# Projection halves issued behind K and Q, context transposes moved to another PSUM bank, and the ScalarE copy of V moved behind a cast

## The chip, the cores and the metric

One core of one Trainium2 chip runs the whole program. The metric is device time in microseconds of that core, as the median of several executions. The engines are TensorE (PE), VectorE (DVE), ScalarE (ACT), GpSimd (POOL), and SyncE (SP), which only issues DMAs here. Each engine works through its own list of instructions strictly in the order in which the program wrote them, and meets the others only at semaphores.

## The reference

The block is a gated cross-attention followed by a gated mixture of experts, over 8 batches of 256 tokens with 128 features. Only the parts that the kernel's order of work depends on are shown.

```
xn = layernorm(layernorm(x))                         # x: (8, 256, 128)
q  = xn @ w_q                                        # 16 heads of 64
k, v = split(ctx_1024 @ w_kv)                        # ctx_1024: (8, 512, 128)
attn = softmax(q * 64**-0.5 @ k.T)                   # per batch and head: 256 x 512
x  = x + tanh(g_xattn) * tanh(gate) * (attn @ v @ w_out + b_out)
t  = layernorm(x)                                    # router, one expert of 8, at most 160 tokens each
x  = x + tanh(g_ffn) * prob * relu(t @ w1[e]) @ w2[e]
```

## The kernel before

Attention runs batch by batch (8), and in a batch pair of heads by pair of heads (8 pairs). One pair is one **slot** of the loop; in the code a slot is `hp`, 0 to 7, and `j` counts slots over all batches. What follows calls them slot 0 to slot 7 of a batch. Each engine has its own function `batch(b)` that writes its instructions for every slot, and those lists are the order of work: nothing is scheduled beyond them.

In slot j, TensorE computes the scores of pair j for two query tiles into two double banks, `psAB` and `psCD` (L1274, or L1267 for the pairs that use a plain fp32 copy: slots 0, 2 and 7). It projects K and Q of pair j+2 into `psEF` (L1193 to L1195), transposes the normalised output of pair j-3 into the end of `psEF` (L1310), projects one eighth of V into `psX` (the same lines), and multiplies values for pair j-2 into `psO` (L1299 to L1301). VectorE takes row maxima (L913, L916), ScalarE the exponentials (L753) and a cast of them to 16 bits (L763), GpSimd the low half of that cast (L654), and SyncE's queue transposes both halves by DMA into `PT` (L477), which the values read two slots later.

Splitting into high and low parts runs through the kernel: ScalarE copies the high part out of PSUM (`kq_hi` L715, `v_hi` L720, `ctxt_hi` L706), and VectorE subtracts it to give the low part (`kq_lo` L900 or L896, `v_lo` L906, `ctxt_lo` L887). `kq_hi` may only start once the transposes L1310 of its slot are done, since they share a bank.

Once per batch there is further work, placed at a fixed slot: the output projection of the batch before in two halves (`project_part` L1353 in slot 1, `project` L1389 in slot 3, both into `psO`, added up on VectorE by `add_part` L957 and `add_attention` L946), the transposes of the next batch's context (`ctx_transposes` L1219, end of slot 2, into `psX`), of the next batch's tokens (slot 4), and the router of the batch before (`tok_transposes` slot 5, `logits` slot 6, `ranks` slot 0 of the batch after, all in `psO`).

`psO` and `psX` each hold one thing at a time. TensorE's `wait_o` and `wait_x` keep for each bank the semaphore that says when its last contents have been read, and make the next writer wait for it: after `project_part` the values wait for `add_part`, after `values` the next writer waits for `normalise_heads` (L924, L930), after a V projection the next waits for `v_lo`. In the program before, VectorE's order in slots 1 and 3 puts `kq_lo` ahead of `add_part` and `add_attention`.

After the last batch's slots comes the rest of the attention and the expert stage, some 50 us.

Of the kernel before, what the change touches and what calls it, by code (L numbers as in the profile page):

```python
# [21 lines left out]
F32 = mybir.dt.float32  # L22
# [11 lines left out]
def gated_block(nc, x, ctx_1024, g_xattn, g_ffn, ln_gamma, ln_beta, w_q, w_kv, w_out, b_out, gate,  # L34
# [34 lines left out]
    with ExitStack() as ctx:  # L69
# [120 lines left out]
        psO = pb("psO", [P, 512])  # L190
        psX = pb("psX", [P, 512])

        def ps_logits(b):
            return (psX if b == B - 1 else psO)[:, 0:QT * E]

        def ps_ranks(b):
            return (psX if b == B - 1 else psO)[:, 0:(QT + 1) * E]

        ps_gw_mid = psO[:, 0:E]

# [114 lines left out]
        def back(b, hp, k):  # L315

            return (b, hp - k) if hp >= k else (b - 1, hp - k + PAIRS)

        def is_last(b):
            return isinstance(b, int) and b == B - 1  # L320
# [65 lines left out]

        def x_bank(b):
            return psO[:, 0:SQ]

        def kq_bank(j):  # L390

# [296 lines left out]
        def _(act):  # L688
# [14 lines left out]

            def ctxt_hi(b):
                act.wait_ge(ctxt_psum, b + 1)
                act.activation(cT_hi[:, b % 2, :], psX[:], ACT.Copy).then_inc(ctxt_hi_done, 1)  # L706

            def kq_hi(b, hp):
                j = b * PAIRS + hp
# [72 lines left out]

            def batch(b):
                for j, hp in slots(b):
                    if hp == CTX_STEP + 1 and not is_last(b):
                        ctxt_hi(b + 1)
                    exps(b, hp, 0)
                    if not (is_last(b) and hp + AHEAD >= PAIRS):
                        kq_hi(*next_pair(b, hp, AHEAD))
                    if hp == CTX_STEP:  # L790
                        v_hi(*v_group(b, hp))
                    if j < LAST:
                        phi(b, hp, 0)
                    exps(b, hp, 1)
                    if ot_pair(j) >= 0:
                        ot_copy(ot_pair(j))
                    if hp != CTX_STEP and v_group(b, hp):
                        v_hi(*v_group(b, hp))
                    if j < LAST:
                        phi(b, hp, 1)  # L800
                    if hp == X_STEP and not is_last(b):
                        xt_hi(b + 1)
                    if hp == LOGITS_STEP and not is_first(b):
                        router_exp(b - 1)
# [32 lines left out]
        def _(dve):  # L837
# [46 lines left out]

            def ctxt_lo(b):
                dve.wait_ge(ctxt_hi_done, b + 1)
                dve.tensor_tensor(cT_lo[:, b % 2, :], psX[:], cT_hi[:, b % 2, :].bitcast(F32), ALU.subtract).then_inc(ctxt_lo_done, 1)  # L887

            def kq_lo(b, hp):
                j = b * PAIRS + hp  # L890
# [176 lines left out]
            def batch(b):  # L1067
                for j, hp in slots(b):
                    row_max(b, hp, 0)
                    if hp == CTX_STEP + 1:  # L1070
                        if not is_last(b):
                            ctxt_lo(b + 1)
                    elif j and v_group(*back(b, hp, 1)):
                        v_lo(*v_group(*back(b, hp, 1)))
                    if hp == RANKS_STEP and b > 1:
                        take_ranks(b - 2)
                    if hp == X_STEP and not is_last(b):
# [15 lines left out]
                    if j == LAST:  # L1093
                        low_parts()
                        place(B - 2)
                    if not (is_last(b) and hp + AHEAD >= PAIRS):
                        kq_lo(*next_pair(b, hp, AHEAD))
                    if hp == CTX_STEP:
                        v_lo(*v_group(b, hp))
                    if hp == PART_STEP and not is_first(b):  # L1100
                        add_part(b - 1, b - 1)
                    if hp == PROJECT_STEP and not is_first(b):
                        add_attention(b - 1)
                    if VALUES_BEHIND <= j < LAST:
                        normalise_heads(*back(b, hp, VALUES_BEHIND))
                    if hp == PROJECT_STEP and not is_first(b):
# [84 lines left out]
        def _(pe):  # L1191
# [22 lines left out]

            def ctx_transposes(b):
                pe.wait_ge(ctx_in, 16 * b + 16)
                wait_x((ctxt_lo_done, b + 1))
                for kt in range(KT):
                    last = pe.transpose(psX[:, P * kt:P * kt + P], ctx_raw[:, kt, :], ident[:])  # L1219
                last.then_inc(ctxt_psum, 1)  # L1220

            def k_project(b, hp):
# [96 lines left out]
                last.then_inc(tokt_psum, 1)  # L1319

            def logits(b):
                (wait_x if b == B - 1 else wait_o)((route, b * ROUTE + 4))
                pe.wait_ge(tokt_done, b + 1)
                pe.wait_ge(gw_mid_done, 1)
                for q in range(QT):
                    last = pe.matmul(ps_logits(b)[:, E * q:E * q + E], tT[:, P * q:P * q + P], gw_mid[:], start=True, stop=True)
                last.then_inc(logit_psum, 1)
# [29 lines left out]
            def ranks(b):  # L1357


                (wait_x if b == B - 1 else wait_o)((route, b * ROUTE + 7))  # L1360
                pe.wait_ge(hot_done, QT * (b + 1))
                if b:
                    pe.wait_ge(route, (b - 1) * ROUTE + 7)
                else:
                    pe.wait_ge(pool_consts, 5)
                carried = taken[:].unsqueeze(1).to_broadcast([P, QT + 1, E])
                pe.matmul(ps_ranks(b).rearrange("p (t e) -> p t e", e=E), ident[:], carried, start=True, stop=False)
                for i, (counts, c) in enumerate(((tri, 2), (ones_bf, 1), (ones_bf, 0))):
                    last = pe.matmul(ps_ranks(b), counts[:], hot_padded[:, c:c + QT + 1, :].rearrange("p t e -> p (t e)"),
                                     start=False, stop=(i == 2))  # L1370
                last.then_inc(pos_psum, 1)
# [51 lines left out]
            def batch(b):  # L1423
                for j, hp in slots(b):
# [6 lines left out]
                        ranks(b - 2)  # L1431
                    if j == LAST:
                        ranks(b - 1)
                    if hp == PART_STEP and not is_first(b):
                        project_part(b - 1, range(PAIRS // 2))
                    if hp == PROJECT_STEP and not is_first(b):
                        project(b - 1)
                    if hp == X_STEP and not is_last(b):
                        x_transposes(b + 1)
                    if hp == TOKT_STEP and not is_first(b):  # L1440
# [5 lines left out]
                    if ahead:  # L1446
                        if is_first(b) and hp == 2:
                            pe.wait_ge(w_lo_rest_done, 3)
                        k_project(*next_pair(b, hp, AHEAD))
                        q_project(*next_pair(b, hp, AHEAD))  # L1450
                    if ot_pair(j) >= 0:
                        if not ahead:
                            pe.wait_ge(kq_done, LAST + 1)
                            pe.wait_ge(ot_done, ot_pair(j))
                        o_transposes(ot_pair(j))
                    if v_group(b, hp):
                        v_project(*v_group(b, hp))
                    if VALUES_BEHIND <= j < LAST:
                        values(*back(b, hp, VALUES_BEHIND))
                    if hp == CTX_STEP and not is_last(b):  # L1460
                        ctx_transposes(b + 1)
                    if j == 0:
                        pe.wait_ge(v_lo_done, 2)
                        keep_busy(6, psO[:, 0:P])
                if is_last(b):
# [5 lines left out]
                    pe.wait_ge(ot_done, LAST - 2)  # L1471
                    o_transposes(LAST - 2)
                    values(b, PAIRS - 2)
                    project_part(b, range(PAIRS // 2, PAIRS - 2), psEF)
                    pe.wait_ge(ot_done, LAST - 1)
                    o_transposes(LAST - 1, psEF[:, 512:1024], 2)
# [112 lines left out]
```

## Time and profile before

| what | value |
|---|---|
| device time, median of 3 (lowest to highest) | 491.48 us (490.69 to 491.77) |
| the profiled execution | 489.88 us, of which its span is 487.9 us |
| TensorE matmul busy | 433.6 us, 89% |
| VectorE, ScalarE, GpSimd busy | 75%, 78%, 73% |
| DMA queue 1, all hardware DMAs | 281600 packets, 77.96 MB, 89.7% of 16 engines |
| granted TensorE clock, mean of the span | 0.994 |

The profile is one execution, so its own time is 1.6 us below the median. A busy share says how full an engine is over the whole span, not whether the end waits for it; where an engine sat idle, the profile names what ended the idle time. In a timeline row the first number is the start in us from the start of the span, the second the time it took, and a bracket gives the idle time just before it and what ended it.

### The profile page before, as it was taken

To read this page: it belongs to the slowest core of one execution; us is meant where nothing else is said; L and a number is where in the kernel's file an instruction comes from. 1 tells how busy PE (TensorE), PEld (TensorE's weight loads), DVE (VectorE), ACT (ScalarE), POOL (GpSimd) and SP (SyncE) were. 2 spreads that over 40 slices of the span, in tenths; PEclk is the share of its full clock that TensorE was granted. 3 is DMA by queue.
4 is the path that set the end of the run, shared out by engine and by line. 5 is a ranking of instruction groups with operands and counts; after the bars stand their busy time and mean duration, and the time that the engine had idled before them with its cause. 6 is when DMAs were issued, how large, how long until landed. Compare 5 with 4: busy or idle time off the path is not lost.

```text
span 487.9 us, 13156 instructions
## 1 busy us (share of the span) xinstructions
PE 433.6 (89%) x5096; PEld 334.3 (69%) x5096; DVE 367.0 (75%) x803; ACT 382.9 (78%) x616; POOL 355.7 (73%) x270
## 2 busy tenths in 40 slices
PE   8869998899889998899889989899889989888893
PEld 7647775676667776676667767677667666657893
DVE  4788886699678886789669887689669867785622
ACT  5879997699778988699788987799779986893330
POOL 3785894788867987798867987788778876681325
PEclk9998999999999999999999999999999999999999
DMA  6399999899998999999989999999989997797021
GB/s 181 128 206 174 184 205 156 162 199 196 194 184 179 193 192 170 187 186 202 190 180 176 179 186 184 195 188 196 190 129 177 192 179 138 124 165 163 14 65 44
DMA packets 283037, 82.10 MB, mean 168 GB/s; under 512 B 264387, under 2 KB 280435, under 8 KB 282976
## 3 DMA queue, kind: packets, MB, share of 16 engines
q1 hardware_dynamic: 281600, 77.96, 89.7%
q0 software_dynamic: 1376, 3.30, 2.1%
q8 instruction: 41, 0.67, 0.6%
q14 instruction: 20, 0.16, 0.1%
HBM read 10.83 MB, written 5.14 MB: 33 GB/s over the span
## 4 chain that ended last, share of the span: by engine, by line
PE 53%; DVE 18%; ACT 12%; DMA 7%; issue 6%; POOL 3%; POOLq 0%; SPq 0%; ACTq 0%; DVEq 0%
DVE MXL L913 7%; DMA PT<-PARTS 6%; PE psO L1299 5%; ACT P L753 4%; PE psAB L1267 4%; PE psO L1301 4%; ACT HL L715 4%; PE psO L1300 4%; PE psAB L1274 4%; PE psCD L1274 3%; DVE HL L900 3%; PE psEF L1193 3%; PE psO L1389 3%; PE psO L1353 3%; PE psEF L1195 2%
## 5 line engine op out<-in xcount | busy, mean ns | idle before, releaser
L654 POOL TENSOR_TENSOR PARTS<-P,PARTS 128x1024 f16<-128x1024 f32 x125 | 267.2, 2140 | 78.3 <-ACT PARTS L763 77.6
L763 ACT ACTIVATE PARTS<-P 128x1024 f16<-128x1024 f32 x126 | 135.3, 1074 | 0.8
L1299 PE MATMUL psO<-VH,PT 128*128 128x65 f16 x1008 | 99.6, 195 | 26.6 <-DVE row L946 11.5
L1299 PEld LDWEIGHTS psO<-VH,PT 128*128 128x128 f16 x1008 | 90.9, 98 | 46.6 <-DVE row L946 14.6
L753 ACT ACTIVATE P<-psAB,NB 128x512 f32<-128x512 f32 x128 | 81.5, 694 | 42.4 <-DVE NB L916 41.1
L1300 PE MATMUL psO<-VL,PT 128*128 128x64 f16 x1008 | 99.0, 193 | 0.0
L1301 PE MATMUL psO<-VH,PT 128*128 128x65 f16 x1008 | 98.8, 194 | 0.0
L913 DVE TENSOR_REDUCE MXL<-psAB 128x2 f32<-128x1024 f32 x64 | 78.3, 1223 | 19.5 <-PE psAB L1274 12.3
L1301 PEld LDWEIGHTS psO<-VH,PT 128*128 128x128 f16 x1008 | 92.0, 97 | 0.0
L1300 PEld LDWEIGHTS psO<-VL,PT 128*128 128x128 f16 x1008 | 91.9, 99 | 0.0
L753 ACT ACTIVATE P<-psCD,NB 128x512 f32<-128x512 f32 x128 | 81.0, 692 | 1.5 <-DVE NB L916 0.7
L913 DVE TENSOR_REDUCE MXL<-psCD 128x2 f32<-128x1024 f32 x64 | 77.6, 1213 | 0.2 <-PE psCD L1274 0.2
L900 DVE TENSOR_TENSOR HL<-psEF,HL 128x768 fp32r<-128x768 f32 x41 | 39.2, 955 | 26.5 <-ACT HL L715 24.7
L715 ACT ACTIVATE HL<-psEF 128x768 fp32r<-128x768 f32 x41 | 33.4, 814 | 19.0 <-PE psEF L1310 18.6
L906 DVE TENSOR_TENSOR VL<-psX,VH 128x512 f16<-128x512 f32 x63 | 42.8, 680 | 1.5 <-ACT VH L720 1.5
L1274 PE MATMUL psAB<-HL 64*128 64x512 f32 x252 | 41.2, 432 | 0.8 <-ACT P L753 0.8
L1274 PE MATMUL psCD<-HL 64*128 64x512 f32 x252 | 37.5, 402 | 4.2 <-ACT P L753 4.2
L720 ACT ACTIVATE VH<-psX 128x512 f16<-128x512 f32 x63 | 38.8, 616 | 0.0
L924 DVE RECIPROCAL rden<-psO 128x4 f32<-128x4 f32 x64 | 11.4, 179 | 35.2 <-PE psO L1301 34.6
L1193 PE MATMUL psX<-w_hi,cT_hi 128*128 128x512 f32 x63 | 30.2, 479 | 5.0 <-DVE VL L906 2.6
L742 ACT ACTIVATE OT<-psEF 128x256 f32<-128x256 f32 (+1 forms) x63 | 25.1, 399 | 9.1 <-PE psEF L1310 7.2
L1274 PEld LDWEIGHTS psCD<-HL 64*128 64x128 f32 x252 | 22.5, 186 | 14.3 <-ACT P L753 10.2
(228 smaller groups left out, 876.5 us busy)
## 6 DMA issues: line engine op xcount, KB each, us to landing
ctx_raw<-in_ctx_dram SPq DMA_DIRECT2D x8, 256.0 KB, 3.6
w1s<-in_L_ffn_w_dram SPq DMA_DIRECT2D x8, 256.0 KB, 3.4
w2s<-in_L_ffn_w_dram SPq DMA_DIRECT2D x8, 256.0 KB, 4.4
PT<-PARTS SPq DMA_TRANSPOSE x126, 4.8
experts_table<-zeros POOLq DMA_DIRECT2D x2, 645.0 KB, 4.1
X<-in_x_dram SPq DMA_DIRECT2D x8, 128.0 KB, 4.0
wraw<-in_L_xattn_w_kv_dram SPq DMA_DIRECT2D x4, 256.0 KB, 5.1
out_dram<-row SPq DMA_DIRECT2D x8, 128.0 KB, 2.8
```

The lines of the kernel that those rows point to most:

```text
L654: pool.tensor_tensor(PARTS[:, par, qt, 1], P32[:, par, qt], PARTS[:, par, qt, 0], ALU.subtract).then_inc(plo_done, 1)
L715: act.activation(HL[:, hp % 2, H_KHI:H_KHI + KQ], kq_bank(j)[:, 0:KQ], ACT.Copy).then_inc(kq_hi_done, 1)
L753: last = act.activation(P32[:, par, qt, SK * h:SK * h + SK], score_bank(qt)[:, SK * h:SK * h + SK], ACT.Exp, bias=NB[:, par, qt, h:h + 1])
L763: act.activation(PARTS[:, hp % 2, qt, 0], P32[:, hp % 2, qt], ACT.Copy).then_inc(phi_done[qt], 1)
L900: dve.tensor_tensor(hl[:, H_KLO:H_KLO + KQ], kq_bank(j)[:, 0:KQ], hl[:, H_KHI:H_KHI + KQ].bitcast(F32), ALU.subtract).then_inc(kq_done, 1)
L906: dve.tensor_tensor(VL[:, kt, 8 * half:8 * half + 8, :], bank[:].rearrange("p (h d) -> p h d", d=DH), VH[:, kt, 8 * half:8 * half + 8, 0:D ...
L913: dve.tensor_reduce(MXL[:, par, qt, :, 0], score_bank(qt)[:].rearrange("p (h n) -> p h n", h=2), AX.X, ALU.max, negate=True).then_inc(max_ ...
L1193: pe.matmul(dst, hi_l, hi_r, start=True, stop=False)
L1274: last = pe.matmul(score_bank(qt)[:, SK * h:SK * h + SK], hl[rows, q + P * qt:q + P * qt + P], hl[rows, k:k + SK], start=(q == H_QHI and k ...
L1299: pe.matmul(psO[:, g:g + DH + 1], phi, VH[:, kt, head, 0:DH + 1], start=first_, stop=False)
L1300: pe.matmul(psO[:, g:g + DH], phi, VL[:, kt, head, :], start=False, stop=False)
L1301: last = pe.matmul(psO[:, g:g + DH + 1], plo, VH[:, kt, head, 0:DH + 1], start=False, stop=last_)
```

## The change

TensorE issues the two projection halves (slots 1 and 3) behind the K and Q projections of the slot rather than ahead of them, and VectorE adds each half ahead of `kq_lo` rather than behind it. The context transposes move from the end of slot 2 to just behind the scores of that slot, and for every batch but the first they go to `psO` rather than `psX`; ScalarE's and VectorE's split of them moves from slot 3 to slot 2. ScalarE's `v_hi` moves behind the cast L763 of the second query tile in every slot, also in slot 2, where it stood between `kq_hi` and the first cast; VectorE's `v_lo` for slot 2 moves to slot 3 as in the other slots. The logits and ranks of the last batch but one go to `psEF`.

```diff
+        def route_bank(b):
+            return {B - 1: psX, B - 2: psEF}.get(b, psO)
...
+        def ctx_bank(b):
+            return psO if b else psX
...
@@ ScalarE, batch(b) @@
-                    if hp == CTX_STEP + 1 and not is_last(b):
+                    if hp == CTX_STEP and not is_last(b):
                         ctxt_hi(b + 1)
                     exps(b, hp, 0)
...
-                    if hp == CTX_STEP:
-                        v_hi(*v_group(b, hp))
...
-                    if hp != CTX_STEP and v_group(b, hp):
-                        v_hi(*v_group(b, hp))
                     if j < LAST:
                         phi(b, hp, 1)
+                    if v_group(b, hp):
+                        v_hi(*v_group(b, hp))
...
@@ VectorE, batch(b) @@
                     row_max(b, hp, 0)
-                    if hp == CTX_STEP + 1:
-                        if not is_last(b):
-                            ctxt_lo(b + 1)
-                    elif j and v_group(*back(b, hp, 1)):
+                    if j and v_group(*back(b, hp, 1)):
                         v_lo(*v_group(*back(b, hp, 1)))
+                    if hp == CTX_STEP and not is_last(b):
+                        ctxt_lo(b + 1)
...
-                    if not (is_last(b) and hp + AHEAD >= PAIRS):
-                        kq_lo(*next_pair(b, hp, AHEAD))
-                    if hp == CTX_STEP:
-                        v_lo(*v_group(b, hp))
                     if hp == PART_STEP and not is_first(b):
                         add_part(b - 1, b - 1)
                     if hp == PROJECT_STEP and not is_first(b):
                         add_attention(b - 1)
+                    if not (is_last(b) and hp + AHEAD >= PAIRS):
+                        kq_lo(*next_pair(b, hp, AHEAD))
...
@@ TensorE @@
-                wait_x((ctxt_lo_done, b + 1))
+                (wait_o if b else wait_x)((ctxt_lo_done, b + 1))
...
-                (wait_x if b == B - 1 else wait_o)((route, b * ROUTE + 4))
+                if b == B - 2:
+                    pe.wait_ge(kq_done, LAST + 1)
+                else:
+                    (wait_x if b == B - 1 else wait_o)((route, b * ROUTE + 4))
...
-                    if hp == PART_STEP and not is_first(b):
-                        project_part(b - 1, range(PAIRS // 2))
-                    if hp == PROJECT_STEP and not is_first(b):
-                        project(b - 1)
+                    if hp == CTX_STEP and not is_last(b):
+                        ctx_transposes(b + 1)
...
                         q_project(*next_pair(b, hp, AHEAD))
+                    if hp == PART_STEP and not is_first(b):
+                        project_part(b - 1, range(PAIRS // 2))
+                    if hp == PROJECT_STEP and not is_first(b):
+                        project(b - 1)
...
-                    if hp == CTX_STEP and not is_last(b):
-                        ctx_transposes(b + 1)
...
+                    pe.wait_ge(route, (B - 2) * ROUTE + 7)
                     project_part(b, range(PAIRS // 2, PAIRS - 2), psEF)
```

## Rows read from the trace of the kernel before

**Rows 1.** Busy time by stretch: slot 1, slot 3, and one whole batch.

```profile
core 0: us, PE busy (x) PEld busy (x) DVE busy (x) ACT busy (x) POOL busy (x), PEclk, DMA share, GB/s
...
177.20:186.00 8.80, 7.15 (x90) 5.96 (x87) 5.59 (x10) 7.08 (x13) 7.42 (x5) 1.00 1.05 181
...
192.90:201.70 8.80, 7.15 (x90) 5.96 (x89) 4.62 (x7) 7.07 (x13) 7.04 (x5) 1.00 1.15 172
...
sum 54.20, PE 49.43 PEld 37.27 DVE 43.14 ACT 45.93 POOL 43.48; mean PE 6.18 PEld 4.66 DVE 5.39 ACT 5.74 POOL 5.43
```

**Rows 2.** Who waited for whom: total us, times, longest.

```profile
PE psO L1299 <- DVE row L946: 11.5, 7, 1.7
PE psO L1299 <- DVE X L957: 11.5, 7, 1.7
...
PE psX L1219 <- DVE VL L906: 3.9, 6, 0.7
...
PE psO L1299 <- DMA PT<-PARTS: 1.7, 4, 0.7
...
PEld psO L1299 <- DVE winners L994: 1.4, 1, 1.4
```

**Rows 3.** Timeline of TensorE, slot 1 of batch 3.

```profile
177.20 0.97 PE L1274 MATMUL psAB<-HL 64*128 64x512 f32 x6
...
178.01 0.86 PE L1274 MATMUL psCD<-HL 64*128 64x512 f32 x6
...
178.80 2.05 PE L1353 MATMUL psO<-wo,OT 128*128 128x128 f32 x16
...
180.60 0.47 PE L1193 MATMUL psEF<-cT_hi,w_hi 128*128 128x512 f32 x1
...
181.88 0.47 PE L1193 MATMUL psX<-w_hi,cT_hi 128*128 128x512 f32 x1
...
184.47 0.20 PE L1299 MATMUL psO<-VH,PT 128*128 128x65 f16 x1 [1.65 <-DVE X L957]
```

**Rows 4.** Timeline of VectorE, the same slot 1.

```profile
183.06 0.96 DVE L900 TENSOR_TENSOR HL<-psEF,HL 128x768 fp32r<-128x768 f32 x1 [1.51 <-ACT HL L715]
183.93 0.47 DVE L957 SCALAR_TENSOR_TENSOR X<-psO,gscale,X 128x256 f32<-128x256 f32 x1
```

**Rows 5.** Timeline of ScalarE, slot 1 and the first exponential of slot 2.

```profile
182.22 0.81 ACT L715 ACTIVATE HL<-psEF 128x768 fp32r<-128x768 f32 x1 [1.29 <-PE psEF L1310]
...
183.87 1.26 ACT L753 ACTIVATE P<-psCD,NB 128x512 f32<-128x512 f32 x2
...
188.63 1.26 ACT L753 ACTIVATE P<-psAB,NB 128x512 f32<-128x512 f32 x2 [1.80 <-DVE NB L916]
```

**Rows 6.** Timeline of TensorE and ScalarE, the context's transposes and copy.

```profile
192.33 0.63 PE L1219 MATMUL psX<-ident,ctx_raw 128*128 128x128 f32 x4 [0.65 <-DVE VL L906]
...
194.25 0.64 ACT L706 ACTIVATE cT_hi<-psX 128x512 fp32r<-128x512 f32 x1
```

**Rows 7.** Timeline of ScalarE, VectorE and TensorE in slot 5: one group of V.

```profile
208.90 0.63 ACT L720 ACTIVATE VH<-psX 128x512 f16<-128x512 f32 x1
...
210.02 0.68 DVE L906 TENSOR_TENSOR VL<-psX,VH 128x512 f16<-128x512 f32 x1
...
211.19 0.47 PE L1193 MATMUL psX<-w_hi,cT_hi 128*128 128x512 f32 x1
```

**Rows 8.** Timeline of SyncE's DMA queue, batches 3 and 4, merged.

```profile
191.59 1.19 SPq L452 DMA_DIRECT2D X<-in_x_dram  x1
...
199.43 0.94 SPq L484 DMA_DIRECT2D ctx_raw<-in_ctx_dram  x1
...
206.11 2.48 SPq L457 DMA_DIRECT2D w1s<-in_L_ffn_w_dram  x2
...
216.03 0.58 SPq L448 DMA_DIRECT2D out_dram<-row  x1
216.71 10.97 SPq L477 DMA_TRANSPOSE PT<-PARTS  x4
...
228.41 16.96 SPq L477 DMA_TRANSPOSE PT<-PARTS  x6
```

More of the change, by code:

```diff
@@ L191, in gated_block @@
         psX = pb("psX", [P, 512])
+        def route_bank(b):
+            return {B - 1: psX, B - 2: psEF}.get(b, psO)
         def ps_logits(b):
-            return (psX if b == B - 1 else psO)[:, 0:QT * E]
+            return route_bank(b)[:, 0:QT * E]
         def ps_ranks(b):
-            return (psX if b == B - 1 else psO)[:, 0:(QT + 1) * E]
+            return route_bank(b)[:, 0:(QT + 1) * E]
         ps_gw_mid = psO[:, 0:E]
@@ L705, in ctxt_hi @@
                 act.wait_ge(ctxt_psum, b + 1)
-                act.activation(cT_hi[:, b % 2, :], psX[:], ACT.Copy).then_inc(ctxt_hi_done, 1)
+                act.activation(cT_hi[:, b % 2, :], ctx_bank(b)[:], ACT.Copy).then_inc(ctxt_hi_done, 1)
             def kq_hi(b, hp):
@@ L886, in ctxt_lo @@
                 dve.wait_ge(ctxt_hi_done, b + 1)
-                dve.tensor_tensor(cT_lo[:, b % 2, :], psX[:], cT_hi[:, b % 2, :].bitcast(F32), ALU.subtract).then_inc(ctxt_lo_done, 1)
+                dve.tensor_tensor(cT_lo[:, b % 2, :], ctx_bank(b)[:], cT_hi[:, b % 2, :].bitcast(F32), ALU.subtract).then_inc(ctxt_lo_done, 1)
             def kq_lo(b, hp):
@@ L1216, in ctx_transposes @@
                 pe.wait_ge(ctx_in, 16 * b + 16)
-                wait_x((ctxt_lo_done, b + 1))
+                (wait_o if b else wait_x)((ctxt_lo_done, b + 1))
                 for kt in range(KT):
-                    last = pe.transpose(psX[:, P * kt:P * kt + P], ctx_raw[:, kt, :], ident[:])
+                    last = pe.transpose(ctx_bank(b)[:, P * kt:P * kt + P], ctx_raw[:, kt, :], ident[:])
                 last.then_inc(ctxt_psum, 1)
@@ L1357, in ranks @@
             def ranks(b):
-                (wait_x if b == B - 1 else wait_o)((route, b * ROUTE + 7))
+                if b == B - 2:
+                    pe.wait_ge(route, b * ROUTE + 4)
+                else:
+                    (wait_x if b == B - 1 else wait_o)((route, b * ROUTE + 7))
                 pe.wait_ge(hot_done, QT * (b + 1))
```

## The prediction, made blind

> **What bounds the kernel now.** I read the busy time by stretch first, then the waits, then the timelines of single slots. A batch takes 54.20 us and TensorE's matmuls fill 49.43 of it at full clock [rows 1], so 4.8 us per batch is all that a better order alone can win. Most of the gap sits in two slots: slots 1 and 3 last 8.80 us each with 7.15 us of matmul, the slots that hold a projection half [rows 1]. The waits name the cause: in seven batches the values wait 1.65 us for `add_part` and as long for `add_attention`, 23.0 us together, and six times the context's transposes wait for `v_lo`, 3.9 us [rows 2].
>
> The timeline of slot 1 shows how that wait comes about. TensorE issues scores, the half, K and Q, the output transposes, V, and then stands until 184.47 [rows 3]. The half was done at 180.85, but VectorE had `kq_lo` first in its list, and that stood 1.51 us for ScalarE's `kq_hi` [rows 4], which stood 1.29 us for the output transposes [rows 5]. So `add_part` started 3.1 us after its operand was there, and held `psO` until 184.40. Slot 3 is built alike.
>
> **The change part by part.** I walk the new order through batch 3, keeping each stretch from start to start as the rows have it.
>
> *Halves behind K and Q, sums ahead of `kq_lo`.* From the first score to the next matmul is 1.60 us, the half takes 1.80 to the next start, K to V 1.28 [rows 3], of which the output transposes, which lie just ahead of V, are 0.14 by the order of the list. So K starts at 178.80, the half at 179.94, the output transposes at 181.74 as before, V at 181.88. The half ends at 181.99; VectorE is idle then (from 183.06 less 1.51, 181.55), so `add_part` runs to about 182.55 and costs nothing ahead of a `kq_lo` that still waits for ScalarE until 183.06 [rows 4]. V needs 0.8 us before the values, so they start at 182.67 and not at 184.47: **1.80 us** won in slot 1. The exponential of the second tile keeps its place, 183.87 to 185.13 [rows 5], and the second scores of slot 2, now due at 185.3, just clear it. Nothing is left over there: ScalarE is next in line.
>
> *Context transposes in slot 2, in `psO`.* The wait of 0.65 us goes with the bank [rows 6], because `psO` was emptied by the normalisation after the values end at 184.3, well ahead of the transposes at 186.1. They last 0.63 us. The new place adds two waits. ScalarE's `ctxt_hi` now stands first in slot 2, and behind it stand all its exponentials, `kq_hi` and casts; it starts when the transposes are done (186.8), which is when ScalarE comes free of slot 1, so I cost the wait at nothing and the copy at 0.64 us [rows 6]. The first exponentials of slot 2 then start near 187.4, still 1.2 us earlier than the 188.63 of before [rows 5]. VectorE's `ctxt_lo` (a 128x512 subtraction like the 0.68 us of `v_lo` [rows 7]) stands ahead of the second row maximum; it ends at 188.2, and the values of slot 2, which need the bank, are due at 188.75: covered, with half a microsecond to spare. Bounds: the transposes' wait of 0.65 gained in full, and on the other side the 0.64 us of the copy and 0.68 us of the subtraction paid in full. I take the gain less what ScalarE costs in the next step, since both waits lie under work.
>
> *Slot 3.* Scores start at 190.3 (before: 192.9). Here ScalarE is late: `kq_hi`, the first cast and the second exponentials of slot 2 end at 191.5, so the second scores stand about 0.4 us. The projection half then repeats slot 1: values at 196.2, slot 4 at 197.75 against 201.7 before. The walk wins **3.95 us** by slot 4.
>
> *`v_hi` behind the second cast.* The sum of ScalarE's work before the next exponentials is the same. The cast, and with it GpSimd's subtraction and the DMA transposes, come 0.5 us sooner; `v_lo` comes later. Slot 5 is the tightest: `v_hi` ran 208.90 to 209.53, `v_lo` from 210.02 to 210.70, V from 211.19 [rows 7]. Put behind a cast of about 1.1 us, `v_hi` ends near 210.5, `v_lo` near 211.25, and V waits some 0.15 us. In slot 2 `v_lo` now comes a slot later, and V of slot 3, behind the half, has room. Bounds per slot: nothing (the other slots) to 1.0 us (the whole move). I take 0.25 us per batch, near the slot-5 row. The walk stands at **3.7 us**.
>
> *Last batch but one's logits in `psEF`.* This removes the one wait of 1.4 us for the routing [rows 2]. But the scores of the last slot then wait for the exponentials before them, which hang on VectorE's maxima, so I count nothing (bounds 0 to 1.4). The added waits are old by the time TensorE gets there.
>
> *What is late next: the DMA queue.* SyncE's queue is not touched in its order, but it is asked to do the same in less time. From 216.71 to 245.37 it issued ten transposes with one load between and no gap worth the name: 28.66 / 10 = 2.87 us each [rows 8]. Sixteen of them are 45.9 us, and the other loads of a batch 1.19 + 0.94 + 2.48 + 0.58 = 5.2 us [rows 8]: **51.1 us** of queue in a batch that now takes 54.20. The walk would need 50.5. So the queue gives out first, at 3.1 us; I take **3.0** and leave the last tenth for transposes that land late.
>
> A transpose moves 128 x 2048 two-byte elements, 524 KB, so 2.87 us is 183 GB/s. The Trainium skill, "DMA: Bandwidth & Descriptors", section "Latency and other measured facts", gives an effective 261 GB/s for such transposes. By that, an estimate, one would take 2.0 us, the queue would need 37 us, and the time would be that of the walk alone. This trace does not agree where the queue is full.
>
> *Sum.* Batches 1 to 7 hold the halves: 7 x 3.0 = 21.0 us. In batch 0 the context's split moves too, but V in slot 3 then waits for `v_lo` where it waited for `ctxt_lo`: nothing. The profiled execution is 489.88 us (span 487.9), which gives 468.9; on the median, 491.48 - 21.0 = **470.5 us**.
>
> **The rivals.** *The queue has room after all.* A transpose that is handed over sooner also drains sooner; the waits for transposed data are only 1.7 us in the whole run [rows 2], which speaks for slack. Then the walk holds, 7 x 3.7 to 7 x 3.95: 464 to 465.6 us. The skill's figure above points this way.
>
> *The queue has less room.* In a batch of 54.20 us the queue stands idle only between some loads and the next transpose, as from 192.78 and from 200.37; if only half the 3.1 us can be used before transposes land behind the values, 7 x 1.55 = 11 us: about 480.5, between 476 and 485.
>
> *ScalarE's chain is the bound.* `kq_hi` still waits for the output transposes (1.29 us [rows 5]), now behind the half as before. If only the 1.25 us by which the first exponentials of slot 2 come earlier survive, 7 x 1.25 = 8.8 us: 482.7.
>
> *Slower: V waits in every full slot.* `v_hi` behind the cast moves `v_lo`, which frees `psX` for the next V. Where TensorE has no gap (slots 0 and 4 to 7, 35 of them), a wait of the whole 1.0 us costs 35 us against 21 won: about 505.5. It decides from 0.6 us per slot. Against it: `v_lo` is held by VectorE's row maximum anyway, and slot 5 shows a shift of about half a microsecond with half of slack.
>
> **How the numbers follow.** Forecast (466 to 476) 0.55; queue with room 0.10; queue with less 0.16; ScalarE's chain 0.08; no effect 0.04; slower 0.07. Faster by over 0.2% (1 us, about what a measurement here can tell from no change) is the first four, 0.89; within 0.2%, 0.04; slower, 0.07. The range 463.5 to 484 takes in both ends of the queue and most of ScalarE's case.
>
> **What would show it.** After: no wait of L1299 on L957 or L946, none of L1219; slots 1 and 3 near 7.0 and 7.5 us; a batch near 51 us; the wait of L1299 on `PT` grown from 1.7 us to several, and the queue's transposes back to back over whole batches. If batches stand at 50.5 with no such wait, the queue had room. If `psCD` scores wait for exponentials over 1 us in slots 2 and 3, ScalarE took the gain. If V waits for `v_lo` by over 0.3 us in slots 4 to 7, the moved copy costs what I held small.

## The result, and the profile after

| what | before | after |
|---|---|---|
| device time, median (lowest to highest) | 491.41 us (490.69 to 491.77) | 469.76 us (468.03 to 470.58) |
| ratio, 95% interval | | 0.9557 (0.9527 to 0.9586) |
| the profiled execution, of which its span | 489.88 us, 487.9 us | 469.92 us, 468.1 us |
| TensorE matmul busy | 433.6 us, 89% | 435.2 us, 93% |
| DMA queue 1, share of 16 engines | 89.7% | 95.7% |

The change made the kernel faster by 4.4%; the forecast of 470.5 us missed the median by 0.7 us. The median of before stands on four executions here; the forecast had three of them. TensorE does the same work in less idle time. The waits of TensorE after (total us, times, longest) answer to [rows 2]:

```profile
PE psO L1300 <- DMA PT<-PARTS: 7.5, 11, 1.9
PE psCD L1275 <- ACT P L759: 5.1, 16, 1.4
PE psX L1194 <- DVE VL L910: 2.7, 2, 2.5
```

The two waits for `add_part` and `add_attention`, 23.0 us, and the 3.9 us of the context's transposes are gone. In their place the values wait for transposed data 7.5 us where they waited 1.7. TensorE's timeline of slot 1 of batch 3 after, against [rows 3]:

```profile
170.64 0.96 PE L1275 MATMUL psAB<-HL 64*128 64x512 f32 x6
...
172.23 0.50 PE L1194 MATMUL psEF<-cT_hi,w_hi 128*128 128x512 f32 x1
...
173.38 1.95 PE L1357 MATMUL psO<-wo,OT 128*128 128x128 f32 x16
175.16 0.38 PE L1311 MATMUL psEF<-ident,O 128*128 128x128 f32 x2
175.30 0.48 PE L1194 MATMUL psX<-w_hi,cT_hi 128*128 128x512 f32 x1
...
176.09 0.20 PE L1300 MATMUL psO<-VH,PT 128*128 128x65 f16 x1
```

No row has a bracket: TensorE does not stand once. Counted from the slot's start, half, V and values begin at 2.74, 4.66 and 5.45 us. VectorE in the same slot, against [rows 4]:

```profile
175.36 0.48 DVE L961 SCALAR_TENSOR_TENSOR X<-psO,gscale,X 128x256 f32<-128x256 f32 x1 [0.22 <-PE psO L1357]
176.49 0.96 DVE L904 TENSOR_TENSOR HL<-psEF,HL 128x768 fp32r<-128x768 f32 x1 [0.64 <-ACT HL L721]
```

The sum starts 0.22 us after VectorE came free, as the half ends, and `kq_lo` behind it still waits 0.64 us for ScalarE: the sum costs nothing there. The busy time by stretch, with the columns of [rows 1], for slots 1, 2 and 3 of batch 3 and then for whole batches 2, 4, 5 and 6:

```profile
170.64:177.60 6.96, 6.96 (x90) 5.94 (x87) 5.78 (x10) 5.22 (x9) 5.08 (x5) 1.00 1.13 186
177.60:183.70 6.10, 6.10 (x76) 4.13 (x73) 5.36 (x9) 6.00 (x11) 5.15 (x3) 1.00 1.06 215
183.70:191.25 7.55, 7.26 (x90) 5.87 (x87) 5.51 (x10) 6.05 (x11) 5.99 (x5) 1.00 1.20 183
...
114.40:164.50 50.10, 49.36 (x609) 37.23 (x607) 43.49 (x94) 45.60 (x74) 43.15 (x32) 1.00 1.16 201
215.20:267.70 52.50, 49.51 (x610) 37.27 (x607) 43.48 (x94) 45.46 (x74) 43.06 (x32) 1.00 1.05 190
267.70:320.30 52.60, 49.78 (x608) 37.28 (x607) 43.56 (x94) 45.91 (x74) 43.26 (x32) 1.00 1.10 194
320.30:370.20 49.90, 49.29 (x606) 36.99 (x605) 43.60 (x94) 45.74 (x74) 43.31 (x31) 1.00 1.09 184
```

The slots are as walked. The batches are not alike: two stand near 50 us, which is TensorE full to 99%, and two stand some 2.5 us longer with the same TensorE work. From the first score of a batch to the next batch's, in us (worked out from the timelines):

| batch | 0 | 1 | 2 | 3 | 4 | 5 | 6 | 7 (seven slots) | its slot 7 to the end |
|---|---|---|---|---|---|---|---|---|---|
| before | 51.8 | 53.5 | 53.8 | 54.2 | 53.9 | 54.0 | 53.7 | 47.8 | 53.2 |
| after | 52.4 | 49.9 | 50.1 | 50.7 | 52.5 | 52.6 | 50.0 | 42.8 | 55.1 |
| gain | -0.6 | 3.6 | 3.7 | 3.4 | 1.4 | 1.4 | 3.8 | 5.1 | -1.9 |

### The profile page after: what moved, and what is told of

The parts are those of the page before. It is cut to its first block, busy times and chain, and to the rows that moved or that the text cites. A ratio compares the mean times of both kernels' runs of the same rounds, so it can differ in the third digit from the quotient of the medians.

```text
span 468.1 us, 13156 instructions
## 1 busy us (share of the span) xinstructions
PE 435.2 (93%) x5096; PEld 333.4 (71%) x5096; DVE 370.1 (79%) x803; ACT 382.5 (82%) x616; POOL 355.7 (76%) x270
## 3 DMA queue, kind: packets, MB, share of 16 engines
q1 hardware_dynamic: 281600, 77.96, 95.7%
## 4 chain that ended last, share of the span: by engine, by line
PE 43%; DVE 14%; DMA 12%; ACT 12%; POOL 11%; issue 6%; POOLq 0%; SPq 0%; ACTq 0%; DVEq 0%
DMA PT<-PARTS 11%; POOL PARTS L660 8%; DVE MXL L917 5%; ACT P L759 5%; DVE HL L904 3%; PE psO L1300 3%; PE psAB L1268 3%; PE psCD L1275 3%; PE psO L1302 3%; PE psO L1301 3%; PE psEF L1194 3%; ACT PARTS L769 3%; PE psO L1396 3%; PE psCD L1268 3%; ACT HL L721 2%
## 5 line engine op out<-in xcount | busy, mean ns | idle before, releaser
L1300 PEld LDWEIGHTS psO<-VH,PT 128*128 128x128 f16 x1008 | 90.8, 98 | 27.6 <-issue 14.5
L904 DVE TENSOR_TENSOR HL<-psEF,HL 128x768 fp32r<-128x768 f32 x41 | 39.1, 953 | 11.6 <-ACT HL L721 10.6
L1275 PE MATMUL psCD<-HL 64*128 64x512 f32 x252 | 38.7, 412 | 5.3 <-ACT P L759 5.1
L1275 PEld LDWEIGHTS psCD<-HL 64*128 64x128 f32 x252 | 21.7, 184 | 19.2 <-ACT P L759 15.9
L1194 PE MATMUL psEF<-cT_hi,w_hi 128*128 128x512 f32 x63 | 30.7, 487 | 0.6 <-DVE cT_lo L891 0.6
```

What stands on the lines that cost most here:

```text
L904: dve.tensor_tensor(hl[:, H_KLO:H_KLO + KQ], kq_bank(j)[:, 0:KQ], hl[:, H_KHI:H_KHI + KQ].bitcast(F32), ALU.subtract).then_inc(kq_done, 1)
L1194: pe.matmul(dst, hi_l, hi_r, start=True, stop=False)
L1275: last = pe.matmul(score_bank(qt)[:, SK * h:SK * h + SK], hl[rows, q + P * qt:q + P * qt + P], hl[rows, k:k + SK], start=(q == H_QHI and k ...
L1300: pe.matmul(psO[:, g:g + DH + 1], phi, VH[:, kt, head, 0:DH + 1], start=first_, stop=False)
```

## The experiments

### The three parts alone

**e1_halves_only** is the kernel before with the halves behind K and Q and the sums ahead of `kq_lo`.

```diff
@@ VectorE, batch(b) @@
-                    if not (is_last(b) and hp + AHEAD >= PAIRS):
-                        kq_lo(*next_pair(b, hp, AHEAD))
...
                         add_attention(b - 1)
+                    if not (is_last(b) and hp + AHEAD >= PAIRS):
+                        kq_lo(*next_pair(b, hp, AHEAD))
...
@@ TensorE, batch(b) @@
-                    if hp == PROJECT_STEP and not is_first(b):
-                        project(b - 1)
...
                         q_project(*next_pair(b, hp, AHEAD))
...
+                    if hp == PROJECT_STEP and not is_first(b):
+                        project(b - 1)
```

> Of the change only the projection halves behind K and Q and their sums ahead of kq_lo. The theory that the values' wait on the sums was the loss: the 23.0 us of that wait go almost whole, 7 batches x (1.8 in slot 1 + 1.1 in slot 3, where ScalarE is late), about 20 us: 469 to 473 us, the values' wait on L957 and L946 under 2 us in all. The rival that ScalarE's chain holds the batch: 7 x 1.25 us, 482 to 484 us. Nothing: 491.

Measured: 473.81 us (473.11 to 477.52), ratio 0.9642 (0.9589 to 0.9696); the profiled execution is the slowest, 477.52. Slots 1 and 3 both fell from 8.8 to 6.99 us, 3.6 us per batch from this part alone, and slot 2 stayed at 6.88. TensorE's waits:

```profile
PE psO L1299 <- DMA PT<-PARTS: 11.2, 14, 2.3
...
PE psX L1219 <- DVE VL L906: 3.0, 5, 0.7
```

The sums are not waited for any more; the transposed data are, 14 times, 11 of them in slots 6 and 7. ScalarE's chain did not hold the gain back, so that rival (482.7 us) falls.

**e2_context_only** is the kernel before with the context's transposes behind the scores of slot 2, in `psO`, and its split in slot 2.

```diff
@@ ScalarE, batch(b) @@
-                    if hp == CTX_STEP + 1 and not is_last(b):
+                    if hp == CTX_STEP and not is_last(b):
                         ctxt_hi(b + 1)
...
@@ TensorE @@
-                wait_x((ctxt_lo_done, b + 1))
+                (wait_o if b else wait_x)((ctxt_lo_done, b + 1))
...
                         project(b - 1)
+                    if hp == CTX_STEP and not is_last(b):
+                        ctx_transposes(b + 1)
...
                         values(*back(b, hp, VALUES_BEHIND))
-                    if hp == CTX_STEP and not is_last(b):
-                        ctx_transposes(b + 1)
```

> Of the change only the context transposes behind the scores of slot 2, in psO, with their split in slot 2; the copy of V stays where it was. The values still wait 1.65 us for the sums in slots 1 and 3. If the wait of L1219 for v_lo (0.65 us in six batches) is worth itself: 487 to 488 us. If ScalarE's copy at the head of slot 2 costs what it gains: 491. If it holds up the exponentials behind it by its 0.64 us and more: 492 to 496 us.

Measured: 492.25 us (488.14 to 493.98), ratio 1.0004 (0.9970 to 1.0039): no difference. Slot 2 fell from 6.88 to 5.94 us and slot 3 rose from 8.80 to 9.87. Its waits show where the gain went:

```profile
PE psO L1301 <- DVE X L960: 11.6, 7, 1.7
PE psO L1301 <- DVE row L949: 11.5, 7, 1.7
PE psCD L1276 <- ACT P L756: 10.6, 18, 1.6
```

The waits for the sums are what they were. In slot 3 the second scores now stand 0.8 us for ScalarE's exponentials in each of batches 1 to 6: such waits make 10.6 us in all, against 3.9 in e3, whose context transposes stay where they were.

**e3_vcopy_only** is the kernel before with `v_hi` behind the cast of the second tile, in the slots other than 2.

```diff
-                    if hp != CTX_STEP and v_group(b, hp):
-                        v_hi(*v_group(b, hp))
                     if j < LAST:
                         phi(b, hp, 1)
+                    if hp != CTX_STEP and v_group(b, hp):
+                        v_hi(*v_group(b, hp))
```

> Of the change only ScalarE's v_hi behind the second cast, in all slots but slot 2. By my walk V waits 0.15 to 0.25 us more per batch and the casts come 0.5 us sooner, which nothing was waiting for: 490 to 492.5 us. The rival on the slower side (V waits up to 1.0 us in 35 slots): 500 us and more. If the transposes had been the limit: faster, 486 to 489 us.

Measured: 490.0 us (488.82 to 493.09), ratio 0.9976 (0.9949 to 1.0004). Alone it is too small to tell from nothing; slot 5 went from 5.83 to 5.92 us.

**e4_vcopy_back** is the kernel after with that one step undone, `v_hi` ahead of the cast again, in slot 2 as well.

```diff
+                    if v_group(b, hp):
+                        v_hi(*v_group(b, hp))
                     if j < LAST:
                         phi(b, hp, 1)
-                    if v_group(b, hp):
-                        v_hi(*v_group(b, hp))
```

> The changed kernel with v_hi ahead of the second cast again (in slot 2 too, behind the output copy). If the queue of transposes is what binds now, casts 0.5 us later land 0.5 us later: the values' wait on PT grows from 7.5 to 12 us or more and the time to 473 to 476 us. If the order of TensorE alone binds: 469 to 470 us, or under it by the 0.2 us per batch that V waits.

Measured: 473.88 us (473.07 to 474.57), ratio 0.9647 (0.9593 to 0.9701), 4 us slower than after. The wait of the values:

```profile
PE psO L1300 <- DMA PT<-PARTS: 12.3, 16, 2.0
```

Against 7.5 us after. The same move that did nothing in e3 is worth 4 us once the order of TensorE no longer hides the transposes. And e4, which has halves and context, stands where e1, which has the halves alone, stands: the context's move is not seen in the time.

### Is it the queue that takes the rest?

**e5_half_transposes** is the kernel after with each DMA transpose moving the high half only, and the values reading it twice: the kernel leaves the low half out of the result, and TensorE does the same work.

```diff
-                sp.dma_start_transpose(PT[:, par, qt].rearrange("p s h k n -> p (s h k) n"),
-                                       PARTS[:, par, qt].rearrange("p s n -> p (s n)")).then_inc(pt_in[qt][par], 16)
+                sp.dma_start_transpose(PT[:, par, qt, 0].rearrange("p h k n -> p (h k) n"),
+                                       PARTS[:, par, qt, 0]).then_inc(pt_in[qt][par], 16)
```

> The changed kernel with half the DMA work of the transposes: only the high half of each cast is transposed, and the values multiply the high half twice (the low half is left out of the result). Every other instruction is the same. If the queue of transposes costs what the two slow batches and slots 6, 7 and 0 lost: the values' wait on PT goes from 7.5 us to under 1 us and the time from 469.8 to 463 to 465 us, each batch from 1 to 6 at 49.7 to 50.2 us. If the waits on PT were covered by others behind them: 468 to 470 us.

Measured: 458.87 us (458.57 to 459.93), ratio 0.9361 (0.9315 to 0.9407). No wait for transposed data is left, and batches 1 to 6 all take 49.7 to 49.9 us. Batch 4 of it, busy time by stretch:

```profile
210.30:260.20 49.90, 49.31 (x608) 36.99 (x605) 43.61 (x95) 45.76 (x74) 43.33 (x31) 1.00 0.64 117
```

So the queue costs the changed kernel up to 469.76 - 458.87 = 10.9 us. In the two profiled executions the difference lies in batch 0 (3.9 us), batches 4 and 5 (2.5 and 2.7), batches 1 to 3 (1.1) and behind slot 7 of the last batch (53.7 us here, 55.1 after). Not all of it is the queue's. The last part is mostly the clock (below): e5's one execution with a mean granted clock as low as after's (0.991) took 459.93 us, 9.8 under after. And in batch 0 V waits 2.46 us for `v_lo` after and 0.90 here, for a reason that the last section shows.

**e6_before_half_transposes** does the same to the kernel before.

```diff
-                            phi, plo = pt[:, 0, h, kt, :], pt[:, 1, h, kt, :]
+                            phi, plo = pt[:, 0, h, kt, :], pt[:, int(j == LAST), h, kt, :]
...
```

> The kernel before with the same half of the transposes left out, and the same part of the result. If the queue became a limit only through the change: 489 to 491 us, since before waits 1.7 us on PT in all. If the queue was a limit already: 485 us or less.

Measured: 486.48 us (484.80 to 489.61), ratio 0.9929 (0.9897 to 0.9961). Its full batches stay at 53.7 us. The two kernels with the queue relieved are 486.48 - 458.87 = 27.6 us apart, or 26.1 by the executions with a mean granted clock of 0.995 or more (484.89 and 458.83): that is the gain of the order by itself, 3.81 us in a full batch (53.74 to 49.93) and 4.5 in the last. Against the 21.7 us of the change, 4.4 to 5.9 were lost to a queue that costs more after than before. What it cost before is less certain: 3.5 us by the ratio (1.9 to 5.1), but batches 1 to 6 of e6 are only 0.9 us shorter in all than those of before.

**e7_vcopy_back_half_transposes** is e4 with the halved transposes of e5, the diffs of both together.

> The changed kernel with v_hi ahead of the second cast again, and with half of the transposes (and of the result's low half) left out. If v_hi behind the cast is worth 4 us only because transposes start half a microsecond sooner: no difference to the changed kernel with half the transposes, within 1 us (463 to 465 us). If it is worth something by itself (ScalarE's or GpSimd's order): 3 to 4 us more than that kernel.

Measured: 458.22 us (457.63 to 459.70), ratio 0.9347 (0.9299 to 0.9395), the same as e5. Where the queue has room, the place of `v_hi` is worth nothing: its 4 us in the change are transposes handed over sooner, not work saved on an engine.

### Where the queue loses it

SyncE's queue after, around batch 2 and around batch 4 (a merged row runs from the first start to the last end):

```profile
106.59 10.92 SPq L483 DMA_TRANSPOSE PT<-PARTS  x4
117.56 0.58 SPq L463 DMA_DIRECT2D w1s<-in_L_ffn_w_dram  x1
118.24 17.94 SPq L483 DMA_TRANSPOSE PT<-PARTS  x6
...
136.92 4.92 SPq L483 DMA_TRANSPOSE PT<-PARTS  x2
...
143.19 5.07 SPq L483 DMA_TRANSPOSE PT<-PARTS  x2
148.31 1.49 SPq L463 DMA_DIRECT2D w1s<-in_L_ffn_w_dram  x2
149.90 6.04 SPq L483 DMA_TRANSPOSE PT<-PARTS  x2
...
207.39 11.02 SPq L483 DMA_TRANSPOSE PT<-PARTS  x4
218.46 0.59 SPq L465 DMA_DIRECT2D w2s<-in_L_ffn_w_dram  x1
219.14 18.06 SPq L483 DMA_TRANSPOSE PT<-PARTS  x6
...
237.93 5.31 SPq L483 DMA_TRANSPOSE PT<-PARTS  x2
...
244.92 5.67 SPq L483 DMA_TRANSPOSE PT<-PARTS  x2
250.64 1.13 SPq L465 DMA_DIRECT2D w2s<-in_L_ffn_w_dram  x2
251.87 7.23 SPq L483 DMA_TRANSPOSE PT<-PARTS  x2
```

and TensorE in slot 6 of batch 4, at the first values of either query tile:

```profile
259.68 0.19 PE L1300 MATMUL psO<-VH,PT 128*128 128x65 f16 x1 [0.59 <-DMA PT<-PARTS]
...
261.24 0.20 PE L1300 MATMUL psO<-VH,PT 128*128 128x65 f16 x1 [0.68 <-DMA PT<-PARTS]
```

One gap of 1.05 us stands ahead of 244.92; no other in either stretch is over 0.5 us. The sixteen transposes of a stretch take 44.9 us around batch 2 and 47.3 around batch 4, and the batches differ by the same 2.4. Late are slots 6 (7.25 us; it reads pair 4, whose transposes stand directly behind two weight loads) and 1 (8.31 us; the transposes that it reads stand behind the third). The loads are not the same in the two stretches: those around batch 2 are of `w1`, those around batch 4 and in batch 5 of `w2`, with as many bytes. Behind two of `w1` the next two transposes take 6.04 us, behind two of `w2` 7.23. Whether the kind of load makes the long batches no run separates. What I tried is the loads' place.

**e8_weights_in_slot3** issues all three loads of a batch in slot 3.

```diff
-        PIECES = {3: 2, 6: 1}
+        PIECES = {3: 3}
```

> The changed kernel, with the expert weights' load of slot 6 issued in slot 3 beside the other two. No byte more or less. If the queue is full from slot 5 to slot 1 and has room in slots 2 to 4: less wait on PT, 466 to 469 us. If the queue is simply full over the whole batch: 469 to 471 us. Slower (472) if three loads together hold up the transposes of slots 3 and 4.

Measured: 474.67 us (470.70 to 476.08), ratio 0.9689 (0.9641 to 0.9737). Three loads ahead of the same transposes make slot 6 late in batches 1 to 5 (6.59, 7.68, 6.71, 7.15, 7.76 us); in batch 6, with one load left, it takes 5.66. Batches 2 and 5 are the latest, one with `w1` and one with `w2`. The profiled execution is the fastest, 470.70 us, and its batches 1 to 6 take 307.6 us against 305.7 after; the other four (474.25 to 476.08) had a lower mean granted clock, 0.987 to 0.989 against 0.992. How much of the 4.9 us by which the median lies above after is due to the loads is not shown.

**e9_weights_in_slots12** issues two in slot 1 and one in slot 2.

```diff
-        PIECES = {3: 2, 6: 1}
+        PIECES = {1: 2, 2: 1}
...
```

> The changed kernel with the three expert weight loads of a batch behind the transposes of slot 1 (two) and slot 2 (one), not of slots 3 and 6. No byte more or less. By the trace of the changed kernel the transposes that these loads then hold up are read in slots 4 and 5, with 3 and 1.2 us to spare, where those of slot 3's loads are read in slot 6 with 0.2. If it is the place of the loads that makes slot 6 late: slot 6 back to 5.7 us in all batches, 464 to 467 us. If the queue is simply full: 469 to 471 us.

Measured: 469.38 us (468.35 to 473.92), ratio 0.9591 (0.9530 to 0.9652): not the gain expected. Slot 6 is back at 5.7 us in batches 1, 2, 4 and 5, but slot 5 is late in batches 3 to 5 (6.65, 6.46, 6.87), the batches in which the load of slot 2 is one of `w2`. The place of a load decides which slot waits; it does not take the load out of a queue that is full.

**e10_and_batch0_eased** is e9 with the load of `w_out` ahead of the first transposes, and VectorE's scaling of `b_out` in slot 0 of batch 0 rather than in slot 2.

```diff
-        BO_STEP, BIAS_STEP = 2, 7
+        BO_STEP, BIAS_STEP = 0, 7
...
             sp.dma_start(ctx_raw[:], ctx_t[1]).then_inc(ctx_in, 16)
+            sp.dma_start(wo[:], w_out.rearrange("(c p) n -> p c n", p=P)).then_inc(wo_in, 16)
...
-                    if is_first(b) and hp == WO_STEP:
-                        sp.dma_start(wo[:], w_out.rearrange("(c p) n -> p c n", p=P)).then_inc(wo_in, 16)
```

> As the kernel before in this call, and the load of w_out issued ahead of the first transposes rather than in slot 3 of batch 0, and VectorE's scaling of b_out in slot 0 of batch 0 rather than slot 2, where V waits 2.5 us behind it. Batch 0 goes from 52.4 us to 47 to 49: 3 to 5 us under the kernel before in this call, 460 to 463 us. If batch 0's waits only move on: within 1 us of it.

Measured: 468.22 us (465.43 to 472.93), ratio 0.9513 (0.9459 to 0.9568). Batch 0 fell to 50.0 us (52.4 after, 53.5 in e9), and its wait for `v_lo`, 2.5 us after and 0.9 in e9, is gone, but the values of all batches still wait 7.8 us: most of what I expected did not come.

**e11_weights_early** is e10 with the eight `w1` loads ahead of the first transposes as well, and one `w2` load each in slots 1 and 2 of batches 1 to 4.

```diff
-        PIECES = {1: 2, 2: 1}
+        PIECES = {1: 1, 2: 1}
...
             sp.dma_start(wo[:], w_out.rearrange("(c p) n -> p c n", p=P)).then_inc(wo_in, 16)
+            for piece in range(E):
+                expert_piece(piece)
...
```

> As the kernel before in this call, with the eight loads of w1 also issued ahead of the first transposes, while the queue has nothing else, and w2's one each in slots 1 and 2 of batches 1 to 4. The queue's bytes in the batches fall by 2.1 MB. If the loads between transposes are what is left of the queue's cost: 458 to 461 us, as with half of the transposes. If the transposes alone fill the queue: as the kernel before in this call.

Measured: **463.22 us** (462.94 to 463.46), ratio 0.9438 (0.9406 to 0.9470), faster than both kernels, but short of the 458 to 461 us expected if the loads were all that was left of the queue's cost. Its batches 1 to 6 take 301.5 us together.

**e12_weights_outside** is e11 with the eight `w2` loads behind the last transposes, and seven short matmuls, whose result nobody reads, ahead of and between the last transposes on TensorE.

```diff
-                    if b and hp in PIECES:
-                        ...
...
+            for piece in range(E, 2 * E):
+                expert_piece(piece)
...
+                    keep_busy(3, psX[:, 0:P])
                     last_transposes(0)
+                    keep_busy(4, psX[:, 0:P])
                     last_transposes(1)
```

> As the run with the weights early, with w2's eight loads behind the last transposes instead of between those of batches 1 to 4, so that no expert weight is loaded in a batch; and seven 128-column matmuls of no use on TensorE in its two idle stretches of the last slot, where the clock fell to half for 3.4 us. If the loads are what is left of the queue's cost in a batch: batches 1 to 6 at 49.7 to 50.2 us. If the idle stretches bring the half clock: none from the last slot to the experts, and 1 to 2 us less from there to the end. Both: 459 to 461 us. If the transposes alone are late, and the clock falls anyway: 463 us. Slower (465) if w2 holds up the experts' rows.

Measured: **461.34 us** (460.17 to 463.56), ratio 0.9410 (0.9386 to 0.9434). The wait of the values in e11 and then in e12:

```profile
PE psO L1301 <- DMA PT<-PARTS: 3.7, 7, 1.2
```

```profile
PE psO L1300 <- DMA PT<-PARTS: 4.0, 5, 1.5
```

With no weight load in any batch, transposes still come late five times, by up to 1.5 us, and 2.5 of the 4.0 us lie in batch 0. Batches 1 to 6 together take 305.7 us after, 301.0 in e12 and 299.4 in e5, one profiled execution each: of the 6.3 us that the queue cost there, the weight loads account for 4.7 and the transposes, with the context, token and output transfers still among them, for 1.6. From e11 to e12 these batches gain 0.5 us and the tail 1.4, where e11 has a fall of the clock (below) and e12 none; batches 0 and 7 lose 0.7.

## Why the prediction was right, and where it was not

**The wait and its cause: right.** Both sums left the list of waits, and half, V and values begin 2.74, 4.66 and 5.45 us into slot 1, where the walk had 2.74, 4.68 and 5.47. e1 has this part alone and carries 17.6 of the 21.7 us.

**The walk: right in its sum, and slots 1 to 3 as walked** (7.00, 6.1 and 7.45 predicted, 6.96, 6.10 and 7.55 measured; ScalarE's stall in slot 3 0.4 predicted, 0.29 measured). In the batches where the queue mostly kept up the gain was 3.6, 3.7, 3.4 and 3.8 us, against 3.7; with room in the queue it was 3.81 (e6 against e5).

**The context's move: the step "I take the gain" was a size too large.** It wins 0.8 us in slot 2, but slot 3 takes 7.55 us where e1 shows that the halves alone make it 6.99: 0.25 us per batch remain. In e2, without the halves, nothing remains, and in e4 none of it is seen.

**`v_hi` behind the cast: the wrong sign.** I saw that the transposes come 0.5 us sooner, and charged 0.25 us per batch for V's wait in slot 5; a paragraph later I made the queue the bound, and did not ask what half a microsecond is worth to it. The charge was 0.09 us (slot 5 5.83 to 5.92), and the step is worth 4 us (e4), all of it through the queue (e7).

**The queue as the next bound: right, and right in its mean; wrong in its form.** The step was "51.1 us of queue in a batch", an even floor from ten transposes of one stretch. Batches 1 to 6 average 50.95 us after, but four of them stand at 49.9 to 50.7 and two at 52.5 and 52.6: the 3.0 us that I took per batch is near the mean (2.9) of gains of some 3.6 and gains of 1.4. The duration of a transpose in the queue is no property of the transpose. In its row after (shortest, median, longest ns, from first to last start), in that of e5, and in that of before:

```profile
L483 SPq DMA_TRANSPOSE PT<-PARTS x126: 1317/2752/4421, 23.3 to 419.4; - x126
```

```profile
L483 SPq DMA_TRANSPOSE PT<-PARTS x126: 1231/1233/2558, 23.3 to 409.1; - x126
```

```profile
L477 SPq DMA_TRANSPOSE PT<-PARTS x126: 1315/2228/4022, 23.2 to 440.9; - x126
```

The shortest issue takes 1.2 to 1.3 us, with half the bytes or with all of them; what is above that I read as SyncE standing before a full queue, since half the bytes take it away. It is not SyncE standing for GpSimd: in the trace after, each row starts 0.03 us or more behind the end of the subtraction whose result it moves. My 2.87 us was mostly such standing. The Trainium skill, "Perfetto Trace Analysis", section "DMA Instruction — HWDGE (DVE, Sync)", says that the reported window of such an instruction is that of the issuing, and that the movement of the data is not in the profile; the trace agrees: after, the median row lasts 2.75 us, and the data have landed 5.4 us (median) after a row's start. Only because the queue was full over all of the stretch of [rows 8] did its sum give a rate at all. Over batch 2 after, also full, the DMA engines moved 201 GB/s in all, and 190 in batch 4. The rival built on room in the queue falls, since the values wait 7.5 us and relief of the queue takes up to 10.9 us off the time. The Trainium skill, "DMA: Bandwidth & Descriptors", section "Latency and other measured facts", gives the 261 GB/s that the prediction weighed for transposes with a non-contiguous middle dimension; no batch after reaches it.

**What the sum left out and what cancelled.** Batch 7 gained 5.1 us rather than 3.0: no weight, context or token load stands in its queue, and a stand of 0.65 us for ScalarE in its slot 3 and half of the 1.2 us for the routing in slot 6 went too. Batch 0 lost 0.6 (and more, like with like: before has a fall of the clock there, as shown below, and after has none), and the tail lost 1.9. The gains of the batches, 21.8, less 1.9 make 19.9, the 19.8 us by which the spans differ. So 470.5 is nearer than its steps deserve.

**The tail** lost most of its 1.9 us with the clock. The busy time by stretch after, where the last transposes run on TensorE:

```profile
418.00:422.00 4.00, 3.00 (x28) 2.70 (x27) 3.22 (x11) 3.06 (x5) 1.11 (x2) 0.63 1.12 238
```

and before, first for the same work and then for a stretch of batch 0:

```profile
440.00:444.00 4.00, 3.40 (x65) 3.39 (x66) 3.44 (x11) 2.75 (x4) 1.60 (x3) 1.00 1.12 234
...
34.00:38.00 4.00, 1.61 (x12) 1.05 (x11) 3.96 (x5) 1.50 (x3) 2.65 (x3) 1.00 1.00 192
38.00:42.00 4.00, 4.00 (x57) 3.58 (x58) 1.94 (x6) 4.00 (x7) 2.14 (x1) 0.57 1.25 186
```

The granted clock fell to the lower level (1.2 GHz, against 2.4) for 3.4 us in the tail after, and for as long in batch 0 before, right behind a stretch in which TensorE was busy 1.61 of 4 us. After has the same gap in batch 0 (1.54 of 4 us) and no fall there. From slot 7 of the last batch to the end the kernels with a fall there take 55.1 (after), 54.8 (e10) and 54.9 us (e11), the others whose tail is built alike 53.7 (e4, e5, e7, e8, e9): 1.1 to 1.4 us for a fall, and 0.5 left for the rest. Which gap is answered by a fall I could not settle; e12, with the idle matmuls in the tail, has none and takes 53.5 us, but e1 to e9 have none there either, without them. Nor does a fall belong to a kernel: of e6's ten executions those with a mean granted clock of 0.992 to 0.996 took 484.8 to 486.6 us, those with 0.988 to 0.991 took 488.6 to 489.6. Its price is not settled either, since e11's execution at 0.998 (462.94 us) is only 0.3 to 0.5 us shorter than the three at 0.991.

## What to carry to other kernels

When a bank is held by a sum that stands in its engine's list behind something that waits for another engine, put the sum first and give TensorE other work to run between the product and the next use of the bank. Then ask what was hidden under the wait: halving a transfer on the chip tells in one run what a queue costs at most, and with a full queue it pays to hand transfers over sooner and to take loads out of the stretch, more than to shift them within it. The issuing row of a DMA is not its duration; take a queue's rate from a stretch without gaps, and check whether another stretch gives the same.

## What the runs showed of the hardware

A VectorE operation on 128x128 elements can take eight times its time beside GpSimd. VectorE's scaling of `b_out` and GpSimd's two subtractions after, then the same in e5, then VectorE's scaling in e11, where no long GpSimd operation runs beside it:

```profile
33.42 2.27 DVE L1118 TENSOR_SCALAR bo<-bo,gscale 128x128 f32<-128x128 f32 x1
...
31.22 4.38 POOL L660 TENSOR_TENSOR PARTS<-P,PARTS 128x1024 f16<-128x1024 f32 x2 [1.64 <-DMA PT<-PARTS]
```

```profile
33.43 0.29 DVE L1118 TENSOR_SCALAR bo<-bo,gscale 128x128 f32<-128x128 f32 x1
...
31.24 4.48 POOL L660 TENSOR_TENSOR PARTS<-P,PARTS 128x1024 f16<-128x1024 f32 x2 [1.63 <-ACT PARTS L769]
```

```profile
20.61 0.29 DVE L1119 TENSOR_SCALAR bo<-bo,gscale 128x128 f32<-128x128 f32 x1
```

After, the scaling ends at 35.69, 0.09 us behind the second subtraction (35.60), and `v_lo` behind it holds up V by 2.46 us in slot 3 of batch 0, nearly all of the third wait at the top. In e5 the second subtraction starts 0.05 us behind the scaling, as it does after (0.04), but there VectorE takes 0.29 us, the subtraction 2.23 us rather than 2.14, and V waits 0.90 us. Which of the two stands changed from run to run: the scaling in slot 2 took 2.27 us in before, after, e1, e6 and e8, and 0.29 in e2 to e5, e7 and e9. So part of what e5 gains in batch 0 is this, and not the queue. The Trainium skill, "SBUF — State Buffer", section "Who interferes with whom", says that VectorE's `tensor_scalar` can go through the port pair that it shares with GpSimd, and that whichever issues first then has the pair for its whole instruction while the other stands; the traces agree, 2.27 us against 0.29, and 2.23 for the subtraction where VectorE did not stand.
